# Last layer's second product: half of its groups kept on chip and turned by TensorE

## What is computed

```python
grouped = x.reshape(b, s // g, g, d)                # 128 groups n of 32 tokens
logits = jnp.einsum('bntd,des->bntes', grouped, Wc) + bc
logits = logits + tie
perm = (logits == jnp.max(logits, axis=-3, keepdims=True)).astype(x.dtype)
permuted = jnp.einsum('bntd,bntes->bnesd', grouped, perm)
inner = jax.nn.relu(jnp.einsum('bnesd,esdf->bnesf', permuted, W1) + b1)
result_permuted = jnp.einsum('bnesf,esdf->bnesd', inner, W2) + b2
result = jnp.einsum('bnesd,bntes->bntd', result_permuted, perm)
```

## Time and profile before

| | before |
|---|---|
| median of 3 runs | 1857.89 us (1856.11 to 1858.67) |
| profiled execution, its own time | 1849.57 us |
| its span, first to last instruction | 1847.8 us |
| TensorE busy in the span | 1707.3 us (92%) |
| VectorE, ScalarE, GpSimd busy | 1286.2, 1145.3, 821.8 us |
| mean granted TensorE clock | 0.956 |
| DMA moved | 303.81 MB, mean 164 GB/s |
| second up products begin | 1715.97 us |
| last write of rp_scratch landed | 1782.7 us |

### The profile page before, as it was taken

One profiled execution on the slowest core, in us unless ns is written; L12 is line 12 of the kernel. 1 busy time (PEld: TensorE's weight loads), 2 busy tenths in 40 slices (PEclk: granted clock), 3 DMA queues, 4 the chain that ended last, 5 costly groups with the idle time before them and its releaser, 6 DMA issues.

```text
span 1847.8 us, 41058 instructions
## 1 busy us (share of the span) xinstructions
PE 1707.3 (92%) x15760; PEld 1443.4 (78%) x15760; DVE 1286.2 (70%) x2770; ACT 1145.3 (62%) x2882; POOL 821.8 (44%) x1292
## 2 busy tenths in 40 slices
PE   5799999999999999999999789999999999988648
PEld 4567676679899999999999668888888888867523
DVE  4799998453518888888886687777777777667321
ACT  1477777423357777777775577777777777734210
POOL 2235442110103333333330677888888887644000
PEclk7799999999999999999999899999999999999766
DMA  7756565256966666666676522222223221112799
GB/s 185 212 125 137 131 128 130 72 181 223 317 232 223 242 242 240 242 243 240 244 237 239 193 71 64 69 88 72 66 64 92 70 64 54 43 49 94 267 365 325
DMA packets 140163, 303.81 MB, mean 164 GB/s; under 512 B 14080, under 2 KB 82944, under 8 KB 124736
## 3 DMA queue, kind: packets, MB, share of 16 engines
q1 hardware_dynamic: 116032, 188.68, 33.1%
q0 software_dynamic: 19584, 108.31, 17.2%
q10 hardware_dynamic: 4352, 4.20, 0.7%
HBM read 210.44 MB, written 90.44 MB: 163 GB/s over the span
## 4 chain that ended last, share of the span: by engine, by line
PE 74%; DVE 9%; DMA 7%; POOL 4%; issue 4%; ACT 1%; SPq 1%; DVEq 0%; POOLq 0%; ACTq 0%
PE ps L1250 12%; PE ps L1236 11%; PE ps L1832 5%; PE ps L373 5%; PE ps L219 4%; PE ps L1863 4%; PE ps L1818 4%; PE ps L1852 4%; PE ps L379 3%; PE ps L464 3%; PE ps L440 2%; DMA R<-rp_scratch 2%; DVE NM L592 2%; DMA rp_scratch<-RP 2%; POOL P L209 2%
## 5 line engine op out<-in xcount | busy, mean ns | idle before, releaser
L196 ACT ACTIVATE P<-ps,NM 128x256 f32<-128x256 f32 x512 | 236.2, 481 | 127.5 <-DVE NM L185 127.4
L209 POOL TENSOR_TENSOR P<-P,RS 128x1024 f32<-128x1024 f32 x128 | 242.9, 1903 | 72.5 <-DVE RS L203 72.0
L1236 PE MATMUL ps<-XRP,W1P 128*128 128x256 f32 x1872 | 226.8, 281 | 3.3 <-DVE W1P L1319 3.3
L1236 PEld LDWEIGHTS ps<-XRP,W1P 128*128 128x128 f32 x1872 | 220.1, 190 | 3.6 <-DVE W1P L1319 3.6
L1250 PE MATMUL ps<-W2P,HP 128*128 128x256 f32 x1872 | 221.5, 277 | 0.0
L1250 PEld LDWEIGHTS ps<-W2P,HP 128*128 128x128 f32 x1872 | 218.0, 188 | 0.0
L592 DVE TENSOR_REDUCE NM<-ps 128x2 f32<-128x512 f32 x256 | 164.3, 684 | 35.9 <-PE ps L440 35.1
L690 ACT ACTIVATE PT<-ps 128x512 f32<-128x512 f32 x256 | 139.2, 597 | 67.9 <-PE ps L452 65.4
L185 DVE TENSOR_REDUCE NM<-ps 128x2 f32<-128x512 f32 x256 | 164.5, 684 | 5.8 <-PE ps L1818 4.2
L1170 POOL DMA_INDIRECT WE<-in_we,WIX x39 | 44.6, 1144 | 268.9 <-DVE W1P L1319 208.8
L1279 ACT ACTIVATE HF<-ps,WE 128x256 f32<-128x256 f32 x312 | 129.0, 465 | 43.2 <-PE ps L1236 43.2
(11 more groups left out here) (225 smaller groups left out, 3688.7 us busy)
## 6 DMA issues: line engine op xcount, KB each, us to landing
KS<-k_scratch SPq DMA_DIRECT2D x64, 256.0 KB, 3.1
V<-v_scratch SPq DMA_DIRECT2D x16, 1024.0 KB, 6.3
rp_scratch<-RP SPq DMA_DIRECT2D x16, 1024.0 KB, 8.7
R<-rp_scratch SPq DMA_DIRECT2D x16, 1024.0 KB, 14.0
k_scratch<-KVM SPq DMA_DIRECT2D x52, 256.0 KB, 4.1
QS<-q_scratch SPq DMA_DIRECT2D x96, 128.0 KB, 4.5
v_scratch<-KVM SPq DMA_DIRECT2D x40, 256.0 KB, 3.0
ys_scratch<-YS SPq DMA_DIRECT2D x39, 256.0 KB, 8.1
```

Source lines behind the costliest of these rows:

```text
L196: i = e.activation(self.P[u % 4][:, c, :], PS[SB[n % 3]][:, y * 256:y * 256 + 256], ACT.Exp, bias=self.NM[:, u % 4, c:c + 1], accum_out=se ...
L209: e.tensor_tensor(p, p, self.RS[:, u % 4, :].unsqueeze(2).to_broadcast([128, 4, 256]), ALU.mult).then_inc(self.s_pn, 1)
L1236: m = e.matmul(PS[p][:, hh * 256:hh * 256 + 256], W1P[i % 2][wi][:, cc * 1024 + hc * 128:cc * 1024 + hc * 128 + 128], XRP[i % 2][xi][:, cc ...
```

## The change

The groups of batches 0 to 7 (kind "a") go as before: groups on partitions, eviction into RPA (two buffers), 1 MB to DRAM, eight writes and eight reads (into three buffers R2A) instead of sixteen each. `down_a` multiplies INT's first 64 columns, as 64-wide weights, with W2; two values of the es range 64 apart use the two halves of the output partitions.

The groups of batches 8 to 15 (kind "b") take another path. `down_b` uses W2 as weights (32 x 128) and INT's columns of 64 groups as the moving side, so channels come out on partitions. The copies `rpb_part` place them in RPB (64 KB per partition, where PX was) so that es lies contiguous for each group and half of the channels. After all downs `turn_b` transposes, for one batch, 16 blocks of 128x128 into four banks SMALL, and VectorE (one) and ScalarE (three) copy them into R2B (two buffers), in the order that R2 had. No DRAM is used.

In the return, `bias` and `back` are the same matmuls as before, but in banks GATHER, biases of two batches ahead of their returns, in the order RET: b0, then b1, a0, b2, a1, ... . The outputs are issued by SP instead of ScalarE's queue, in four buffers XO as before.

The four up products of the second half stand in a row, parts 2, 3, 0, 1 (PARTS): 2 and 3 are still in their two buffers, and 0 and 1 have two more buffers, filled after the last out projection (s_om). So W1 is loaded in six pieces instead of eight. W2 has four buffers; a piece now holds the q that a step of `down_a` and `down_b` shares. Every step k of 8 runs `down_a(k)` (SMALL banks) and `down_b(k)` (GATHER banks).

```diff
...
+    XO = [Arena(nc, x3_at + 2048 * i)(f"XO{i}", [128, 2, 256], fp32) for i in range(4)]
...
-    WF2P.append(Arena(nc, q1_at)("WF2P1", [128, 8, 256], fp32))
+    WF2P += [Arena(nc, q1_at + 8192 * i)(f"WF2P{i + 1}", [128, 8, 256], fp32) for i in range(3)]
+    R2A = [Arena(nc, q1_at + 8192 * i)(f"R2A{i}", [128, 8, 256], fp32) for i in range(NR)]
...
+    R2B = [Arena(nc, w1o_at + 8192 * i)(f"R2B{i}", [128, 8, 256], fp32) for i in range(2)]
+    WF1P += [Arena(nc, ot1_at + 8192 * i)(f"WF1P{i + 2}", [128, 2, 32, 32], fp32) for i in range(2)]
+    RPA = [Arena(nc, ot1_at + 8192 * i)(f"RPA{i}", [128, 2, 4, 256], fp32) for i in range(2)]
+    PX = Arena(nc, attn_at)("PX", [128, 2, 128, 64], fp32)
+    RPB = Arena(nc, attn_at)("RPB", [128, 2, 64, 128], fp32)
...
+    PARTS = ((0, 1, 2, 3), (2, 3, 0, 1))
...
+    RET = [x for i in range(10) for x in ((("b", i - 1),) if 1 <= i <= 8 else ()) + ((("a", i - 2),) if i >= 2 else ())]
...
+    def rpa_free(w, k):
+        if k >= 2:
+            w.wait_ge(d_ks_rp[(k - 2) % 4], ks_sent + 16 * ((k - 2) // 4 + 1))
+    def rpa_part(k, r):
+        return RPA[k % 2][:, :, r, :], PS[SMALL[r]][:, :].rearrange("p (h d) -> p h d", h=2)
+    def rpb_part(k, r):
+        es = 16 * (4 * (k % 2) + k // 2) + r
+        return (RPB[:, :, :, :].rearrange("p a g s -> p s (a g)")[:, es:es + 13:4, :],
+                PS[GATHER[r]][:, :].rearrange("p (q n) -> p q n", q=4))
...
+    def pe_up(e, w, hf, x):
+        j = PARTS[hf][x]
+        buf = j + 2 if hf and j < 2 else j % 2
+        if buf < 2:
+            w.wait_ge(d_kl_wf1[buf], kl_sent + 16 * (j // 2 + 1))
+        else:
+            w.wait_ge(d_wf1[j], 16)
...
-        def down(q2):
-            w.wait_ge(d_wt_wf2[q2 // 4 % 2], wt_sent + 16 * (q2 // 8 + 1))
...
+        def down_a(k):
+            second_in(k // 2)
+            w.wait_ge(s_in, 8)
             w.wait_ge(s_rb, 32)
             w.wait_ge(s_x3e, 16)
             w.wait_ge(s_pm, 48)
             w.wait_ge(s_pb, 16)
-            w.wait_ge(s_e0, taken_of(q2))
-            w.wait_ge(s_e1, taken_of(q2))
-            w.wait_ge(s_in, 16 if q2 >= 4 else 0)
-            for q in (2 * q2, 2 * q2 + 1):
-                for r in range(4):
-                    rows = slice(32 * r, 32 * r + 32)
-                    m = e.matmul(PS[DOWN[down_set(q2)][r]][:, q % 2 * 256:q % 2 * 256 + 256], INT[rows, q, :],
-                                 WF2P[q // 8 % 2][rows, q % 8, :], start=True, stop=True)
+            w.wait_ge(s_e0, 2 * k - 1)
+            w.wait_ge(s_e1, 2 * k - 1)
+            for h in range(2):
+                for a in range(2):
+                    for r in range(4):
+                        rows = slice(32 * r, 32 * r + 32)
+                        m = e.matmul(PS[SMALL[r]][64 * a:64 * a + 64, h * 256:h * 256 + 256],
+                                     INT[rows, 16 * a + 2 * k + h, 0:64],
+                                     WF2P[k // 2][rows, 4 * a + 2 * (k % 2) + h, :], start=True, stop=True)
             m.then_inc(s_fm, 1)
...
+        def down_b(k):
+            w.wait_ge(s_in, 16)
+            w.wait_ge(s_e0, 2 * k)
+            w.wait_ge(s_e1, 2 * k)
+            for ql in range(4):
+                for dh in range(2):
+                    for r in range(4):
+                        rows = slice(32 * r, 32 * r + 32)
+                        c0 = (2 * ql + dh) * 64
+                        m = e.matmul(PS[GATHER[r]][:, c0:c0 + 64], WF2P[k // 2][rows, 4 * (k % 2) + ql, dh * 128:dh * 128 + 128],
+                                     INT[rows, 16 * (k % 2) + 4 * (k // 2) + ql, 64:128], start=True, stop=True)
+            m.then_inc(s_fm, 1)
+        def turn_b(i):
+            for t in range(4):
+                w.wait_ge(s_e0, 16)
+                w.wait_ge(s_e1, 16)
+                if i and t == 0:
+                    w.wait_ge(s_e0, 16 + i)
+                elif i:
+                    w.wait_ge(s_e1, 16 + 3 * (i - 1) + t)
+                for u in range(2):
+                    for dh in range(2):
+                        c0 = u * 256 + dh * 128
+                        m = e.transpose(PS[SMALL[t]][:, c0:c0 + 128], RPB[:, dh, 8 * i + 2 * t + u, :], ident)
+                m.then_inc(s_fm, 1)
+        def bias(kind, b):
+            n = returned(kind, b)
+            M, tok = PS[GATHER[(n - 1) % 4]], 256 * (b + 8 * (kind == "b"))
+            w.wait_ge(s_xo, n - 4)
             w.wait_ge(s_b2, 2)
...
+        def back(kind, b):
+            n = returned(kind, b)
+            M, tok = PS[GATHER[(n - 1) % 4]], 256 * (b + 8 * (kind == "b"))
+            if kind == "a":
+                R = R2A[b % NR]
+                w.wait_ge(d_r2[b % NR], 16 * (b // NR + 1))
+            else:
+                R = R2B[b % 2]
+                w.wait_ge(s_e0, 16 + b + 1)
+                w.wait_ge(s_e1, 16 + 3 * b + 3)
+            for lt in range(2):
+                for g in range(4):
+                    c0 = tok + lt * 128 + 32 * g
...
+        for x in range(4):
+            pe_up(e, w, 1, x)
+        for k in range(8):
+            down_a(k)
+            down_b(k)
+        for i in range(10):
+            if i < 8:
+                turn_b(i)
+            if 1 <= i <= 8:
+                bias("b", i - 1)
+            if i >= 2:
+                bias("a", i - 2)
+            if 1 <= i <= 8:
+                back("b", i - 1)
+            if i >= 2:
+                back("a", i - 2)
...
+            t, m = 2 * (b + 8 * (kind == "b")), (n - 1) % 4
+            w.wait_ge(s_cm2, n)
+            w.wait_ge(d_x_wf2_out[m], 16 + 16 * ((n - 1) // 4))
+            e.tensor_tensor(flat(XO[m][:, :, :]), flat(X[:, t:t + 2, :]), PS[GATHER[m]][:, :], ALU.add).then_inc(s_xo, 1)
+        for x in range(4):
...
             for r in range(2):
-                i = e.tensor_copy(RP[out_at(q2)][:, :, r, :], PS[DOWN[down_set(q2)][r]][:, :].rearrange("p (q d) -> p q d", q=2))
+                i = e.tensor_copy(*rpa_part(k, r))
             i.then_inc(s_e0, 1)
-            if q2 < 2:
-                dve_up(e, w, 1, q2 + 2)
-        for b in range(16):
-            w.wait_ge(s_cm2, b + 1)
-            w.wait_ge(d_x_wf2_out[b % 4], 16 + 16 * (b // 4))
-            e.tensor_tensor(flat(XO[b % 4][:, :, :]), flat(X[:, 2 * b:2 * b + 2, :]), PS[b % 8][:, :], ALU.add).then_inc(s_xo, 1)
+            w.wait_ge(s_fm, 2 * k + 2)
+            for r in range(2):
+                i = e.tensor_copy(*rpb_part(k, r))
+            i.then_inc(s_e0, 1)
+        for i in range(10):
+            if i < 8:
+                w.wait_ge(s_fm, 16 + 4 * i + 1)
+                r2b_free(w, i)
+                e.tensor_copy(*turned_part(i, 0)).then_inc(s_e0, 1)
+            if 1 <= i <= 8:
+                out_add("b", i - 1)
+            if i >= 2:
+                out_add("a", i - 2)
...
+            w.wait_ge(s_fm, 2 * k + 2)
+            for r in range(2, 4):
+                i = e.activation(*rpb_part(k, r), ACT.Copy)
+            i.then_inc(s_e1, 1)
+        for i in range(8):
+            r2b_free(w, i)
+            for t in range(1, 4):
+                w.wait_ge(s_fm, 16 + 4 * i + t + 1)
+                e.activation(*turned_part(i, t), ACT.Copy).then_inc(s_e1, 1)
...
+        def first(j, buf):
+            sent = d_kl_wf1[buf] if buf < 2 else d_wf1[j]
+            e.dma_start(WF1P[buf][:, :, :, :], A["wf1"][:, :, 32 * j:32 * j + 32, :]).then_inc(sent, 16)
...
-            e.dma_start(WF2P[j % 2][:, :, :], A["wf2"][:, 8 * j:8 * j + 8, :]).then_inc(d_wt_wf2[j % 2], 16)
+            sent = d_wt_wf2[j] if j < 2 else d_wf2[j - 2]
+            e.dma_start(WF2P[j][:, :, :].rearrange("p (a q) d -> p a q d", a=2),
...
+        def out(kind, b):
+            n = returned(kind, b)
+            t, m = 2 * (b + 8 * (kind == "b")), (n - 1) % 4
+            w.wait_ge(s_xo, n)
+            e.dma_start(o_v[:, t:t + 2, :], XO[m][:, :, :]).then_inc(d_x_wf2_out[m], 16)
+        def back_in(b):
+            w.wait_ge(s_cm2, returned("a", b - NR) if b >= NR else 0)
+            e.dma_start(R2A[b % NR][:, :, :], rpd[8 * b:8 * b + 8, :, :].rearrange("n s d -> s n d")).then_inc(d_r2[b % NR], 16)
         w.wait_ge(s_ca, 64)
...
+        first(0, 0)
+        first(1, 1)
+        w.wait_ge(s_om, 32)
+        first(0, 2)
+        first(1, 3)
+        w.wait_ge(s_u3, 1)
+        first(2, 0)
+        w.wait_ge(s_u3, 2)
+        first(3, 1)
         w.wait_ge(s_ga, 16)
         second(0)
         second(1)
-        first(6)
-        first(7)
-        for q2 in range(16):
-            w.wait_ge(s_e0, q2 + 1)
...
+        for k in range(8):
+            w.wait_ge(s_e0, 2 * k + 1)
+            w.wait_ge(s_e1, 2 * k + 1)
+            e.dma_start(rpd.rearrange("g (a k y) d -> k a g (y d)", a=2, k=8)[k],
+                        RPA[k % 2][:, :, :, :].rearrange("p h r d -> p (h r d)")).then_inc(d_ks_rp[k % 4], 16)
...
-        w.wait_ge(s_u3, 8)
...
-            w.wait_ge(s_cm2, b - NR + 1)
```

(62 more changed lines are left out.)

71 lines of the change are left out of this document (24 added, 47 removed).

## The result

The changed kernel takes 1946.8 us (median of 4 runs, 1940.5 to 1950.0) against 1857.0 us (4 runs, 1854.1 to 1858.7): ratio 1.048, 95% interval 1.045 to 1.051. It is 90 us slower, where 40 us less were forecast. The profiled execution took 1947.04 us, span 1945.2.

A forecast was written before the change was run, and what follows sets the result against it. The tail's writes and reads were taken as bound by bytes through DRAM; the new tail, TensorE-bound at full clock, summed 1725.7 + 30.4 + 1.4 + 15.4 + 31.2 + 3.4 = 1807.5 in the span, 40 us less: 1818, range 1808 to 1840.

The forecast's parts named there:

- the price of a step: Second-half downs: down_b 2.1 plus down_a 1.7 make 3.8 us per step, eight 30.4; copies and 1 MB write hidden.
- The second case: RPA writes in the downs land in 8.7 us, a step takes 5.0 instead of 3.8: 1828 us; chance 0.09.
- The only such case: Low clock from the first up product to the end: 23 us slower, median 1881; chance 0.04.
- Ups: Four second-half up products in a row, first 3.4 us at low clock, others 2.1 each: 9.7, to 1725.7.
- Downs with eviction: Eight steps of down_b and down_a, 30.4 us, plus 1.4 us evicting the last RPB parts, to 1757.5.
- no dearer than a plain one: Copies into RPB in the downs: priced from the PX copy that scatters pairs, 0.69 us.
- the third case: Low clock in the downs: a step takes 6.7 us, eight 53.6, 23 more: 1841 us; chance 0.09.
- down_a's price: Downs: 1.7 us per down_a, bounds 1.45 and 2.3, from old downs, three taking 5.09 us at the low clock.
- Return: After the downs: turns 15.4 us plus bias and return of 16 batches 31.2 us, together 46.6.
- the fourth case: Low clock in the return stage: 82.9 us instead of 46.6, median 1854; chance 0.06, wholly or in part.
- the rule on transposes: Return stage: transposes wouldn't count as activity for the clock, so it would stay low and end 36 us later.
- the high level from the second up product to the end: Tail: TensorE's clock expected at 1.00 throughout, as in attention and at 1688.8 to 1709.2.

The follow-up runs named there:

- a_split: The changed kernel with each write into rp_scratch issued as two DMAs of 64 partitions: 1838.2 us against 1855.9 before, ratio 0.991.
- a_esmajor: a_split with RPB laid out es first, so copies write 512-byte runs and transposes gather single values: 1840.3 us against 1862.1 before, ratio 0.988.

## Why the prediction was wrong

*The step that failed* is in the paragraph on the price of a step: "the write of 1 MB 2.7 us at 387 GB/s" and "for one at a time I take 5" for the landing. Both were carried over from writes of the kernel before, with the size as the only thing compared. The target's new order of dimensions makes it 19.6 us, and eight of them 157. The second case, "writes bind", had the right mechanism and the right sign (the RPA copies wait for rp_scratch), but it took 8.7 us to land, the median of a row that didn't have the new shape, where 37.8 were measured. The range was too narrow for the same reason: no case slower than the kernel before was about a transfer. The only such case was the clock. The clock was low here too (0.50 in the window above), but TensorE was busy for 29% of it and waited for the writes.

*With that one edit undone* (a_split), the other steps can be read. Tail forecast 91.5 us from the first up product, measured 115.8:

- Ups: 9.7 forecast, 20.0 measured. 7.6 us are holes. They also stand in the trace of before (2.17 us ahead of 1722.20, with no releaser), where I had read the time between the products as waits for other work. The rest is the low clock, to which TensorE falls back in the holes. A term for instruction fetches was missing from the sum.
- Downs with eviction: 31.8 forecast, 49.3 measured. down_b at 2.0 and down_a at 1.1 us were right or cheaper at the high clock. Wrong was the copy into RPB, "no dearer than a plain one": 1.23 us each while both engines copy, not 0.69. The row for PX writes pairs, RPB single values at twice the distance. A step became down_b plus its copies, 4.7 us at the high clock (the first one). And the clock was 0.50 from 1752.1 to 1799.9, so 6.36: the third case, with a chance of 0.09, happened, though its step was put at 6.7. It fell after TensorE had waited 1.61 us for copies. One reading behind down_a's price was off without consequence: the three old downs of 5.09 us weren't wholly at the low clock (granted 0.59 in that stretch).
- Return: 46.6 forecast, 42.7 measured. An iteration takes 4.71 us (1.90 turns, 0.95 biases, 1.86 returns), not 5.8: run in long blocks, bias and return of a batch cost 1.4, outside my lower bound of 1.7. 1.83 us of waiting for the last read is in it.
- End: 3.4 forecast, 3.8 measured.

(The sum of the fourth case is 1843.8 us as it stands, not 1844.0.)

So of the 40 us, a_split keeps 16 in the tail (18 in the median): 10.3 are lost in the ups and 17.5 in the downs, while the return gives 3.9 more than forecast.

*The clock and the rule on transposes.* In a_split the turns begin at the low clock, and TensorE does nothing but transposes from 1794.30 to 1800.47. Two windows, columns as above:

```profile
1794.30:1799.70 5.40, 5.40 (x26) 5.40 (x27) 1.38 (x2) 1.80 (x4) 0.00 (x0) 0.50 0.59 174
1800.00:1835.00 35.00, 34.14 (x407) 25.80 (x405) 13.24 (x20) 10.83 (x21) 0.00 (x0) 1.00 0.96 312
```

The clock rises at 1799.9, with only transposes since 1794.3 (the first bias product begins at 1800.47), and stays at 1.00 until 1837, when TensorE's last work is done. The changed kernel shows it without any product shortly before: TensorE was idle for over 15 us, did transposes alone, and the clock rose at 1872.0, with the first bias product at 1872.98. Its windows:

```profile
1851.50:1867.10 15.60, 0.00 (x0) 0.00 (x0) 3.03 (x4) 2.86 (x4) 0.00 (x0) 0.50 0.13 54
1867.20:1871.90 4.70, 4.70 (x22) 4.70 (x23) 0.84 (x2) 1.79 (x3) 0.00 (x0) 0.50 0.14 59
1872.10:1882.00 9.90, 6.44 (x71) 4.93 (x69) 2.32 (x4) 3.15 (x6) 0.00 (x0) 1.00 0.13 55
```

So the fourth case fell, and the rule of the Trainium skill, "TensorE: Matmul & The Clock Gate", Part 4, that the prediction quoted against the change does not hold here. For the downs the expectation "the high level from the second up product to the end" was wrong. a_esmajor, whose steps are shorter, held 1.00 for the first two thirds of them and 0.50 for the rest (windows):

```profile
1753.00:1776.00 23.00, 19.15 (x571) 15.26 (x571) 14.61 (x24) 12.23 (x23) 0.00 (x0) 1.00 0.86 231
1776.00:1787.00 11.00, 10.27 (x184) 8.13 (x168) 5.42 (x10) 4.61 (x10) 0.00 (x0) 0.50 0.89 230
```

It fell at 1776.0, after a hole of 1.45 us (1772.57 to 1774.02).

What stays open: whether the holes alone keep the third RPA buffer from gaining, and why the copies into RPB cost 2.45 us in one place and 1.90 in another.

## What to carry to other kernels

The price of a DMA is that of its shape, not only of its bytes: before a row's rate is used for a new transfer, compare the outermost dimension of its target (the runs here vary the target's), and where a rearrangement puts a small one outermost, split the transfer. A DMA share that sits at a simple fraction (0.13, 0.51) while everything waits for DMA says how many engines are in use. When data takes a new route, each access that scatters single values, on the copying or on the reading engine, needs a price from a row with the same pattern; a row with pairs is another pattern. And a dense run of short matmuls has a price per instruction too: divide its instructions by 256 and look for what a packet of the instruction queue costs, 3.5 to 3.8 us here.

## What the hardware showed that was not expected

- A transfer of 1 MB in 8 KB runs takes 19.6 us with two entries outermost; the rates are 53, 214 and 390 GB/s for 2, 8 and 16, so with sixteen it is some 2.7 us by the rate.
- Evicting 128x512 values as single words 512 bytes apart took 1.23 us on VectorE and ScalarE when both began together and 0.95 when one began 0.25 us earlier; 0.69 and 0.60 in runs of 512 bytes; 1.0 with four neighbours 16 bytes apart innermost.
- A 128x128 transpose that reads its values 512 bytes apart takes 2.55 us for 16, contiguous 1.90.
- Dense short matmuls (16 ns apart) ran into holes without a semaphore, 128 matmuls apart, 1.6 to 1.8 us long with no other transfer and up to 4.2 while 4 MB load. With each goes one 16 KB packet of the instruction queue, 256 instructions; TensorE resumes 1.2 to 1.6 us after it has landed.
- The clock rose from 0.50 to 1.00 while TensorE did nothing but transposes, in a_split after downs and in the changed kernel after more than 15 us without work.
